# The gate's statistics products as pairs of 32-row matmuls in the last stage of an audio tower

## What is computed

```python
h = tok(x)                                   # 32 sequences, 384 tokens each, 256 channels
h = h + attn(layernorm(h))
h = h + ffn(layernorm(h))                    # six gelu experts, two chosen per token

# inside attn: delta rule in chunks, two FIR filters, and a gate that mixes four branches
gate_in = concat([x, stats(fir_short), stats(fir_long), stats(delta_out), stats(v)])   # 256 + 32
logits  = gelu(gate_in @ mlp_w1 + mlp_b1, exact) @ mlp_w2 + mlp_b2                     # 288 -> 512 -> 16
w       = softmax(logits / temp)             # per head, over the four branches
o       = w0*fir_short + w1*fir_long + w2*delta_out + w3*v
# stats(y): mean and standard deviation of each of 4 heads: 8 numbers a branch, 32 in all
```

## Time and profile before

| | |
|---|---|
| median of 3 runs | 2475.34 us (2475.2 to 2481.58) |
| span of the profiled execution, first to last instruction | 2491.3 us (its own time; nothing outside the span is listed) |
| PE busy | 2346.5 us, 94% |
| DVE, ACT, POOL busy | 1893.7, 1346.6, 555.7 us |
| mean granted clock of PE | 0.977 |

### The profile page before, as it was taken

How to read it: one execution, slowest core, us unless ns; L and a number is a source line. 1 busy time by engine, 2 the same in 40 slices (tenths; PEclk the granted TensorE clock), 3 DMA queues, 4 the chain that set the end, 5 groups by cost and what they waited for, 6 DMA issues and landing times.

```text
span 2491.3 us, 54761 instructions
## 1 busy us (share of the span) xinstructions
PE 2346.5 (94%) x21052; PEld 1767.1 (71%) x21052; DVE 1893.7 (76%) x5201; ACT 1346.6 (54%) x2633; POOL 555.7 (22%) x413
## 2 busy tenths in 40 slices
PE   6999999999799689999999999999999999999998
PEld 4666666666588577777777777777777777777775
DVE  4999999999597467667777777777776677667765
ACT  3888888888435244455445444455445444455453
POOL 1444444444300021111111111111111111111111
PEclk9999999999769699999999999999999999999999
DMA  3777776777779432221332123222322223222300
GB/s 94 231 231 248 236 243 220 251 236 234 270 273 345 164 104 80 74 68 68 122 104 69 68 88 107 74 68 68 125 77 93 68 92 104 74 68 68 125 20 20
DMA packets 224321, 334.55 MB, mean 134 GB/s; under 512 B 113984, under 2 KB 190752, under 8 KB 215360
## 3 DMA queue, kind: packets, MB, share of 16 engines
q1 hardware_dynamic: 219744, 309.03, 37.5%
q10 hardware_dynamic: 2304, 12.58, 1.2%
q0 software_dynamic: 2016, 9.44, 1.0%
HBM read 191.68 MB, written 164.23 MB: 143 GB/s over the span
## 4 chain that ended last, share of the span: by engine, by line
PE 47%; DVE 11%; ACT 6%; issue 3%; POOL 0%; DVEq 0%
PE bank L1636 8%; PE bank L1630 7%; PE bank L1569 6%; PE bank L1456 4%; PE bank L1599 4%; PE bank L1579 3%; PE bank L1573 3%; PE bank L1546 2%; PE bank L1489 2%; PE bank L1497 2%; ACT L1770 2%; ACT L1765 1%; DVE c L2029 1%; DVE DL L1981 1%; PE bank L1530 1%
## 5 line engine op out<-in xcount | busy, mean ns | idle before, releaser
L2078 DVE SCALAR_TENSOR_TENSOR v_all<-bank,we,v_all 128x256 f32<-128x256 f32 x576 | 265.1, 476 | 208.6 <-PE bank L1636 203.7
L1636 PE MATMUL bank<-w2e,HE 128*128 128x256 f32 x1152 | 329.6, 394 | 29.4 <-DVE v_all L2078 25.7
L738 DVE SCALAR_TENSOR_TENSOR Y<-bank,convw,Y 128x383 f32<-128x383 f32 (+2 forms) x576 | 330.5, 602 | 4.3 <-ACT Y L626 4.0
L1630 PE MATMUL bank<-v_all,w1e 128*128 128x384 f32 x768 | 286.5, 496 | 0.5 <-ACT HE L1770 0.5
L444 PE MATMUL bank<-pb,wqkv 128*128 128x384 f32 x768 | 284.1, 494 | 1.8 <-DVE Y L738 1.8
L1636 PEld LDWEIGHTS bank<-w2e,HE 128*128 128x128 f32 x1152 | 194.9, 190 | 78.5 <-ACT HE L1770 31.7
L1770 ACT ACTIVATE HE<-bank 128x384 f32<-128x384 f32 x192 | 94.0, 490 | 232.7 <-PE bank L1630 232.0
L1569 PE MATMUL bank<-v_all,w1g 128*128 128x384 f32 x512 | 193.8, 501 | 7.6 <-ACT v_all L1765 7.6
L1630 PEld LDWEIGHTS bank<-v_all,w1e 128*128 128x128 f32 x768 | 136.9, 191 | 75.1 <-issue 19.8
L1748 ACT ACTIVATE first_stage<-bank 32x384 f32<-32x384 f32 (+1 forms) x192 | 88.4, 477 | 175.8 <-PE bank L1556 128.2
L444 PEld LDWEIGHTS bank<-pb,wqkv 128*128 128x128 f32 x768 | 132.7, 192 | 62.1 <-DVE Y L738 8.8
(11 more groups left out here) (211 smaller groups left out, 5374.2 us busy)
## 6 DMA issues: line engine op xcount, KB each, us to landing
packa<-pa SPq DMA_DIRECT2D x32, 1932.0 KB, 6.2
v_all<-packa SPq DMA_DIRECT2D x32, 1932.0 KB, 8.1
packb<-pb SPq DMA_DIRECT2D x32, 768.0 KB, 6.3
v_all<-packb SPq DMA_DIRECT2D x32, 768.0 KB, 10.5
toeplitz<-taps SPq DMA_DIRECT2D x128, 190.0 KB, 5.4
toep<-toeplitz SPq DMA_DIRECT2D x32, 760.0 KB, 7.8
packb<-fsk SPq DMA_DIRECT2D x32, 384.0 KB, 2.9
first_stage<-fl SPq DMA_DIRECT2D x32, 384.0 KB, 8.7
```

What stands on the lines that cost most here:

```text
L738: dve.scalar_tensor_tensor(out=Y[:, j, lag:T], in0=proj_bank[j][:, 0:T - lag], scalar=convw[:, j, CK - 1 - lag:CK - lag], in1=Y[:, j, lag: ...
L1630: mm = pe.matmul(bank[6][:, 0:T], w1e[:, a, k, :], YT[s][:, a, :], start=(a == 0), stop=(a == HALF - 1))
L1636: pe.matmul(expert_bank(b), HE[k % 2][:, b * P:(b + 1) * P], w2e[:, k, :], start=True, stop=True)\
L2078: dve.scalar_tensor_tensor(out=HA[s][:, b, :], in0=expert_bank(b), scalar=we[s][:, b, k:k + 1], in1=HA[s][:, b, :], op0=ALU.mult, op1=ALU. ...
```

## The change

The 32 statistics are written twice side by side (64 columns of `SGM`), so that the transpose puts them on rows 0 to 31 and on rows 32 to 63 of `SGT`. `w1s` holds the weights of the even blocks m on rows 0 to 31 and those of the odd blocks on rows 32 to 63. `gate_s(it, pair)` issues two matmuls one after the other, of 32 rows each, on different rows and into different banks. In the queue of PE `gate_s` 0 stands behind `gate_x` 1 and ahead of `merge_b`, and `gate_s` 1 behind `gate_x` 3. ACT does `gelu_gate` 0 and 1 ahead of `copy_merge_b` and `copy_merge_c`, and 2 and 3 behind them. DVE and ACT each write the second copy of the statistics with one more instruction a step. The clears of `w1s` and `SGT` in the second stage are gone, and the weights come in two transfers instead of one.

```diff
-    w1s = sb("w1s", [P, MLP])
+    w1s = sb("w1s", [2 * GATE_S, MC // 2, P])
...
-        load(tail["w1s"][0:GATE_S, :], w["mlp_w1"][D:])
+        for q in range(2):
+            load(tail["w1s"][q * GATE_S:(q + 1) * GATE_S, :, :],
+                 w["mlp_w1"][D:].rearrange("k (m q c) -> k m q c", q=2, c=P)[:, :, q, :])
...
-                        clear(tail["w1s"][SC:2 * SC, :], slice(SC, 2 * SC), MLP)
-                        clear(tail["w1s"][DH:P, :], slice(DH, P), MLP)
...
-                        clear(tail["SGT"], slice(0, P), T)
...
+        def statistics(which, copy):
+            return SGM[:, :, copy, :].rearrange("p b (r m h) -> p r m b h", r=4, m=2)[:, :, which, :, :]
...
-                        mm = pe.transpose(bank[5][0:GATE_S, b * P:(b + 1) * P],
-                                          SGM[:, b, :, :, :].rearrange("p r m h -> p (r m h)"), ident[:, :])
+                        mm = pe.transpose(bank[5][0:2 * GATE_S, b * P:(b + 1) * P], SGM[:, b, :, :].rearrange("p q s -> p (q s)"),
+                                          ident[:, :])
...
-                def gate_s(it, m):
+                def gate_s(it, pair):
                     pe.wait_ge(*sgT_copied.now(it))
-                    pe.matmul(mlp_bank[m][:, 0:T], w1s[:, m * P:(m + 1) * P], SGT[:, :], start=False, stop=True)\
-                        .then_inc(mlp_ready.sem, 1)
+                    for q in range(2):
+                        rows = slice(q * GATE_S, (q + 1) * GATE_S)
+                        pe.matmul(mlp_bank[2 * pair + q][:, 0:T], w1s[rows, pair, :], SGT[rows, :], start=False, stop=True,
+                                  skip_group_check=True).then_inc(mlp_ready.sem, 1)
...
                         gate_x(it, it % 2, 0)
-                        gate_s(it, 0)
...
                         gate_x(it, it % 2, 1)
+                        gate_s(it, 0)
...
-                        gate_s(it, 1)
                         gate_x(it, it % 2, 2)
-                        gate_s(it, 2)
...
                         gate_x(it, it % 2, 3)
-                        gate_s(it, 3)
+                        gate_s(it, 1)
...
-                    act.activation(SGM[:, :, :, 1, :].rearrange("p b r h -> p r b h"),
-                                   var[:, :, :].rearrange("p r (b h) -> p r b h", b=BLK), ACT.Sqrt).then_inc(std_ready.sem, 1)
+                    for q in range(2):
+                        ins = act.activation(statistics(1, q), var[:, :, :].rearrange("p r (b h) -> p r b h", b=BLK), ACT.Sqrt)
+                    ins.then_inc(std_ready.sem, 1)
...
                         gelu_gate(it, 0)
+                        gelu_gate(it, 1)
                     if 0 <= n < NB:
                         copy_merge_b(n)
-                    if 0 <= it < NB:
-                        gelu_gate(it, 1)
+                        copy_merge_c(n)
+                    if 0 <= it < NB:
                         gelu_gate(it, 2)
-                    if 0 <= n < NB:
-                        copy_merge_c(n)
-                    if 0 <= it < NB:
                         gelu_gate(it, 3)
...
-                    dve.tensor_copy(SGM[:, :, :, 0, :].rearrange("p b r h -> p r b h"),
-                                    found[:, :, 1::3].rearrange("p r (b h) -> p r b h", b=BLK)).then_inc(mean_ready.sem, 1)
+                    for q in range(2):
+                        ins = dve.tensor_copy(statistics(0, q), found[:, :, 1::3].rearrange("p r (b h) -> p r b h", b=BLK))
+                    ins.then_inc(mean_ready.sem, 1)
```

More of the change, by code:

```diff
@@ L981, in load_third_phase_weight @@
         load(tail["w2e"][:, :, :], w["ffn_w2"].rearrange("e p n -> p e n"))
-WEIGHT_LOADS = 11
-CLEARED = 3 + 7
+WEIGHT_LOADS = 12
+CLEARED = 3 + 4
 FIRST_DONE = 16 * (1 + NE + 2)
-FACTORS_CLEARED = 3 + 4
+FACTORS_CLEARED = 3 + 2
 CONSTANTS = 2 + NE - 1
@@ L1098, in between @@
                         act.activation(tail["r12"][:, NH:2 * NH], tail["m12"][:, 0:NH], ACT.Ln).then_inc(setup_act, 1)
-                    if g == 2 and j == 3:
-                        act.wait_ge(loaded, 16 * WEIGHT_LOADS)
-                        clear(tail["w1s"][SC:2 * SC, :], slice(SC, 2 * SC), MLP)
-                        clear(tail["w1s"][DH:P, :], slice(DH, P), MLP)
                     if g == 2 and j == 4:
@@ L1361, in third_phase @@
         tail.update(signals=signals, fl_stored=fl_stored, before_e=before_e, minus_half=minus_half,
-                    s12=s12, r12=r12, m12=m12, bv=bv, SGT=SGT, UF=[u.rearrange("p m c -> p (m c)") for u in UF],
+                    s12=s12, r12=r12, m12=m12, bv=bv, UF=[u.rearrange("p m c -> p (m c)") for u in UF],
                     TL=TL.rearrange("p m d -> p (m d)"), S=S.rearrange("p m d -> p (m d)"))
@@ L1376, in third_phase @@
         ST = sb("ST", [P, 4, NM // 2, 6])
-        SGM = sb("SG", [P, BLK, 4, 2, NH])
+        SGM = sb("SG", [P, BLK, 2, GATE_S])
         var = sb("var", [P, 4, NM])
@@ L1568, in gate_x @@
                     for a in range(HALF):
-                        pe.matmul(mlp_bank[m][:, 0:T], w1g[:, a, m * P:(m + 1) * P], chans(pb[s], PX)[:, a, :], start=(a == 0), stop=False)
-                def gate_s(it, m):
+                        pe.matmul(mlp_bank[m][:, 0:T], w1g[:, a, m * P:(m + 1) * P], chans(pb[s], PX)[:, a, :],
+                                  start=(a == 0), stop=False, skip_group_check=True)
+                def gate_s(it, pair):
                     pe.wait_ge(*sgT_copied.now(it))
-                    pe.matmul(mlp_bank[m][:, 0:T], w1s[:, m * P:(m + 1) * P], SGT[:, :], start=False, stop=True)\
-                        .then_inc(mlp_ready.sem, 1)
+                    for q in range(2):
+                        rows = slice(q * GATE_S, (q + 1) * GATE_S)
+                        pe.matmul(mlp_bank[2 * pair + q][:, 0:T], w1s[rows, pair, :], SGT[rows, :], start=False, stop=True,
+                                  skip_group_check=True).then_inc(mlp_ready.sem, 1)
                 def gate_out(it, b):
@@ L1777, in deviations @@
                     act.wait_ge(*vmax_ready.now(it))
-                    act.activation(SGM[:, :, :, 1, :].rearrange("p b r h -> p r b h"),
-                                   var[:, :, :].rearrange("p r (b h) -> p r b h", b=BLK), ACT.Sqrt).then_inc(std_ready.sem, 1)
+                    for q in range(2):
+                        ins = act.activation(statistics(1, q), var[:, :, :].rearrange("p r (b h) -> p r b h", b=BLK), ACT.Sqrt)
+                    ins.then_inc(std_ready.sem, 1)
                 def copy_stats(it):
                     act.wait_ge(*sgT_ready.now(it))
-                    copy(SGT[0:GATE_S, :], bank[5][0:GATE_S, 0:T]).then_inc(sgT_copied.sem, 1)
+                    copy(SGT[0:2 * GATE_S, :], bank[5][0:2 * GATE_S, 0:T]).then_inc(sgT_copied.sem, 1)
                 def copy_merge_a(n):
@@ L1854, in step @@
                         gelu_gate(it, 0)
+                        gelu_gate(it, 1)
                     if 0 <= n < NB:
                         copy_merge_b(n)
-                    if 0 <= it < NB:
-                        gelu_gate(it, 1)
-                        gelu_gate(it, 2)
-                    if 0 <= n < NB:
                         copy_merge_c(n)
                     if 0 <= it < NB:
+                        gelu_gate(it, 2)
                         gelu_gate(it, 3)
```

## The result

The changed kernel takes 2454.47 us (median of 6 runs, 2446.41 to 2464.86), the kernel before 2477.45 (median of 6, 2472.68 to 2494.14). The ratio is 0.9904, 95% interval 0.9881 to 0.9928: faster by 1.0%. Measured again beside the experiments, the ratio was 0.9890 (0.9864 to 0.9916). The prediction was 2448.0 in a range of 2442 to 2459: the measured time lies in the range, but above the 2443 to 2452 that had been given most of the chance.

What follows compares the result with a forecast made beforehand. PE's queue was taken to bound the third stage. 29 full steps at 0.88 us (25.5) plus 1.8 for three partial steps, 27.3 together, came off 2475.3: 2448.0 us, with an 8-in-10 range of 2442 to 2459.

Steps and rivals of the forecast that it cites:

- The bound: Third stage: PE's queue sets the 50.91 us step, so time taken out ahead of `gate_out` counts unless another engine is late.
- The price of a pair: Two `gate_s` products on different row groups: two slots of 0.323 us, 0.645 together, instead of four slots, 1.29.
- The rival of three slots: In each `gate_s` pair, the second product overlaps only the first one's second pass: 0.56 a full step, 2458 us; chance 0.11.
- The changes of shape: Around each `gate_s` pair: 0.09 us on leaving a tile shape, 0.11 on entering with weights of 128 columns.
- The waits: PE still waits 0.2 us at `gate_x` 2 for gelu 0; `merge_c` has 0.14 slack for the copies of `copy_merge_b`.
- The slack of 0.2 at `merge_a`: `merge_a` moves 0.645 us earlier to 1512.76; its inputs from ACT and DVE are there by 1512.48 and 1512.54.
- no wait of PE at `merge_a`: Sign the prediction listed for its being right: PE does not wait at `merge_a` in the third stage.
- The total: 29 full steps at 0.88 us, 25.5, plus 1.8 for three partial steps: 27.3 off the median 2475.3, giving 2448.0.
- the term for the three partial steps: Steps i = 1, 2 and 32, where part of the work is missing: estimated 0.6 us saved each, 1.8 together.
- the third stage repeats to 0.01 us: Assumed of the third stage, so the 27.3 us saving was taken off the median unscaled.
- the rival that a wait takes part of the gain: Thin slacks at `merge_a` (0.2) and `merge_c` (0.14): lateness of 0.2 to 0.3 us a step, 2454 to 2458; chance 0.12.

## Why the prediction was right

**The bound.** PE sets the step, and time taken out ahead of `gate_out` counts: the 0.90 that vanish between `gate_x` 0 and `merge_d` are the 0.90 of the step, and the wait behind `gate_out` is 0.8 as before.

**The price of a pair.** Two slots, taken from the 64-row products. Shown directly by the shared starts, and by the kernel with both products on the same rows, which loses 0.95. The rival of three slots would have made the second pair 1.17 long; it is 0.85. Each product raises a semaphore with its second pass, which tells the passes apart. On the same rows the second and the fourth of the four records raise it, so the two passes of one product start one behind the other; on different row groups it is the two that start last. So the second product's first pass starts 0.01 behind the first product's first pass and 0.42 ahead of its second one. The rule of strict program order (the Trainium skill, TensorE: Matmul & The Clock Gate, section "The mechanism" of part 3) does not describe these records, if the order in the queue is the one that the same rows show; no trace lists the queue itself.

**The changes of shape.** 0.09 on leaving and 0.11 on entering, predicted and found: the pairs take 0.84 and 0.85, and in the first the two starts and `merge_b` lie 0.43 and 0.41 apart, where a pass is 0.323. The move that takes one change away saves 0.20. A price at each change agrees with the drain that the Trainium skill names (TensorEngine Tiling (Array Packing), section "Key Properties"); that the array drains is not itself seen in a trace. The price is also paid between 32 by 128 and 32 by 32, from the first pair to `merge_b`: `expert_out` (4,2) behind them starts 3.11 after `gate_x` 1, the 2.26 of before and 0.85.

**The waits.** The sum had PE waiting 0.2 for gelu 0 (measured 0.23) and `merge_c` 0.14 ahead of trouble (0.16). At `merge_c` nothing was hidden, as the kernel with the later gelu shows. The slack of 0.2 at `merge_a` held in 28 of the 29 full steps and broke in one, against the sign "no wait of PE at `merge_a`". That step, i = 6, takes 50.20 us in the first profile of the changed kernel and 50.22 in the second. DVE idles between two short instructions of the second norm there, for no reason that the profile shows, and its queue runs 0.28 late: the transposes end 1.77 behind the start of `transpose_stats` instead of 1.49. The transposes on DVE and `merge_a` on PE in the first profile:

```profile
1087.76 0.56 DVE L1901 STREAM_TRANSPOSE first_stage<-first_stage 32x384 f32<-32x384 f32 x1
...
1088.46 0.95 PE L1467 MATMUL bank<-first_stage,v_all 32*32 32x32 f32 x48
```

`merge_a` begins 0.14 behind their end. So much of the 0.2 is the way from DVE to PE, and less than 0.1 was to spare.

**The total.** The step was predicted at 50.03 and is 50.01. What was off is the term for the three partial steps, an estimate of 0.6 each, 1.8 in all. Step i = 2 gave nothing (48.35 to 48.33), and the last one 0.2 (67.47 to 67.26 from its `transpose_stats` to the end). Step i = 1 shows no gain that can be told from its scatter: 39.57 and 39.12 in the two profiles of before, 41.51 and 39.12 in those of the changed kernel. So it is not so either that the third stage repeats to 0.01 us, on which the sum relied; its full steps do, with the exceptions named. PE's timeline in step 2, before the change:

```profile
905.53 0.95 PE L1467 MATMUL bank<-first_stage,v_all 32*32 32x32 f32 x48 [0.41 <-DVE first_stage L1901]
```

and in the changed kernel (second profile):

```profile
886.05 0.95 PE L1467 MATMUL bank<-first_stage,v_all 32*32 32x32 f32 x48 [1.08 <-DVE first_stage L1901]
...
891.90 1.58 PE L1489 MATMUL bank<-first_stage,v_all 64*64 64x64 f32 x24 [0.20 <-ACT first_stage L1749]
```

With no expert work of `f` around it, `merge_a` already waited for DVE's transposes, and the 0.67 taken out ahead of it went into that wait. `merge_c`, with no `expert_out` (5,0) ahead of it, waited another 0.20 for ACT's copies, where it did not wait before. The first is the very wait that had 0.2 of slack in a full step. So the last stage became 26.4 us shorter (1628.2 to 1601.8 from the first `transpose_stats` to the end, the second profile of the changed kernel against the first of before) instead of 27.3. Against its first profile it is 24.1, because step i = 1 took 41.51 there. The measured distance between the medians is 23.0, and its interval spans 18 to 29 us (0.9928 and 0.9881 of 2477.45); the second measurement gave 26.0 (2478.23 to 2452.23). Both agree with the sum. But the median of 2454.47 alone would as well have fitted the rival that a wait takes part of the gain (2454 to 2458); that it does not is read from the step, which kept all of its 0.90.

**What the prediction did not say** is how the gain divides. By the experiments 0.53 of 0.90 is the order, which needs no 32-row products at all: the two passes of `gate_s` 0 stood ahead of the chain to the gelu for which PE waited. 0.37 are the row groups. (The row groups could not be tried in the old order: a pair needs `gate_x` of both of its blocks ahead of it.) Where nothing hides them they are worth 0.90 (two pairs at 0.645, less two shape changes at 0.20); in the order of the change 0.20 of that go into a third shape change and 0.33 into the wait for the gelu with its late weight load.

## What to carry to other kernels

Where an engine waits for a chain that starts at one of its own earlier instructions, first move work from ahead of that start to behind it: here that alone gave more than half of the gain. Products of few rows paid here when they ran in pairs on different row groups and into different banks (one bank for both was not tried). But each change of tile shape costs about 0.2 us in this kernel, so put them beside other tiled work; and ask of each gain whether a wait behind it is going to take it back. To read effects below 1% in a kernel whose early stages scatter, compare the length of a repeated step, not the totals.

## What the runs showed of the hardware

Two float32 products of 32 rows and 384 columns, issued one behind the other on different row groups into different banks, take 0.645 us together, as long as one of them; on the same rows they take 1.29 (0.85 and 1.48 to the next group, less 0.20 for the changes of shape). A product of 32 rows alone takes as long as one of 128 (0.645). A change of the tile shape among 128 by 128, 64 by 128, 64 by 64, 32 by 128 and 32 by 32 cost 0.09 us on leaving a shape, and 0.11 on entering one whose weights have 128 columns. The change from the transposes (128 rows, weights of 32 or 64 columns) to full matmuls cost nothing measurable: three transposes of 128 columns take 0.32 us to the start of `gate_x` with 32 columns of weights (1511.05 to 1511.37 before the change) and 0.33 with 64 (1486.87 to 1487.20 after), as long as one pass of 384 columns. The clock of the second stage differs between executions of the same kernel (0.79 and 0.97 in the same 100 us), and in these two the last stage began 15 us apart.
